# First layer of a four-layer kernel: the shift mask moved into q and k, the bias' third part added on the scores' row groups, and two VectorE steps written for ScalarE

## The reference

```python
B, DIM, HEADS, BLOCKS = (16, 48, 6, 6)
WS, SHIFT, MLP = (8, 4, 4)
...
def _block(x, shifted, n1g, n1b, qkvw, qkvb, pw, pb, rpb, n2g, n2b, f1w, f1b, f2w, f2b):
    shortcut = x
    x = _ln(x, n1g, n1b).reshape(B, H, W, DIM)
    if shifted:
        x = jnp.roll(x, (-SHIFT, -SHIFT), (1, 2))
    xw = _win_part(x)
    qkv = (xw @ qkvw.T + qkvb).reshape(-1, N, 3, HEADS, HD).transpose(2, 0, 3, 1, 4)
    q, k, v = (qkv[0], qkv[1], qkv[2])
    attn = jnp.einsum('bhnd,bhmd->bhnm', q * SCALE, k)
    attn = attn + rpb[RPI].transpose(2, 0, 1)[None]
    if shifted:
        attn = (attn.reshape(B, NW, HEADS, N, N) + MASK[None, :, None]).reshape(-1, HEADS, N, N)
    attn = jax.nn.softmax(attn, -1)
    xw = jnp.einsum('bhnm,bhmd->bnhd', attn, v).reshape(-1, N, DIM)
    xw = xw @ pw.T + pb
    x = _win_rev(xw)
    if shifted:
        x = jnp.roll(x, (SHIFT, SHIFT), (1, 2))
    x = shortcut + x.reshape(B, H * W, DIM)
    h = _ln(x, n2g, n2b)
    h = jax.nn.gelu(h @ f1w.T + f1b, approximate=False) @ f2w.T + f2b
    return x + h
```

## Time and profile before

| | us |
|---|---|
| median of 3 runs | 938.65 |
| the runs | 934.58, 942.16, 938.65 |
| the profiled execution | 939.39 |
| its span | 937.6 |
| TensorE busy | 766.7 (82%) |
| VectorE busy | 796.1 (85%) |
| ScalarE busy | 571.5 (61%) |
| GpSimd busy | 239.9 (26%) |

### The profile page before, as it was taken

How to read it: one execution, slowest core, us unless ns; L and a number is a source line. 1 busy time by engine, 2 the same in 40 slices (tenths; PEclk the granted TensorE clock), 3 DMA queues, 4 the chain that set the end, 5 groups by cost and what they waited for, 6 DMA issues and landing times.

```text
span 937.6 us, 20502 instructions
## 1 busy us (share of the span) xinstructions
PE 766.7 (82%) x7954; PEld 510.5 (54%) x7956; DVE 796.1 (85%) x2014; ACT 571.5 (61%) x854; POOL 239.9 (26%) x276
## 2 busy tenths in 40 slices
PE   2699999999999999999999978889877867432446
PEld 1467887777788777777777753376321111000113
DVE  7899999999989999998999964654449999999983
ACT  1387777787778777786777743133356666555142
POOL 6222222222222223222222221392121121212101
PEclk8699999999999999999999997887876765565577
DMA  8200000000000000002000000100002676657501
GB/s 233 72 2 3 1 2 2 1 2 2 2 2 2 2 2 2 2 2 108 3 2 1 2 1 1 50 1 1 1 1 51 119 140 129 123 114 135 101 0 34
DMA packets 11623, 34.14 MB, mean 36 GB/s; under 512 B 1879, under 2 KB 4359, under 8 KB 11271
## 3 DMA queue, kind: packets, MB, share of 16 engines
q0 software_dynamic: 5904, 21.24, 11.9%
q1 hardware_dynamic: 5623, 11.60, 4.2%
HBM read 10.81 MB, written 0.79 MB: 12 GB/s over the span
## 4 chain that ended last, share of the span: by engine, by line
PE 54%; DVE 30%; issue 5%; ACT 5%; DMA 2%; POOL 2%; POOLq 0%; DVEq 0%; another core or an unknown queue 0%; ACTq 0%
PE narrow L1524 7%; PE wide L1445 4%; PE scores_a L1505 4%; PE scores_b L1505 3%; DVE prod L1007 3%; DVE prod L1015 3%; PE last L1603 3%; PE wide L1589 3%; PE narrow L1554 2%; DVE mx L613 2%; PE last L1576 2%; PE narrow L1457 2%; DVE v L607 2%; PE scores_a L1494 2%; PE scores_a L1481 2%
## 5 line engine op out<-in xcount | busy, mean ns | idle before, releaser
L381 POOL TENSOR_TENSOR stb<-stb,neg_half 128x4 f32<-128x4 f32 x48 | 48.4, 1008 | 329.0 <-DVE stb L678 329.0
L1524 PEld LDWEIGHTS narrow<-v,pt 128*64 128x64 f32 x2304 | 82.1, 142 | 16.2 <-issue 16.2
L1133 ACT ACTIVATE d<-d 128x768 f32<-128x768 f32 x96 | 80.8, 841 | 16.4 <-DVE d L625 15.7
L1524 PE MATMUL narrow<-v,pt 128*64 128x54 f32 x2304 | 88.4, 229 | 0.0
L1787 PE MATMUL scores_b<-xb,gates_w 128*32 128x512 bf16 x192 | 26.0, 556 | 62.0 <-DVE yo L1027 52.9
L1149 ACT ACTIVATE ga<-wide 128x512 f32<-128x512 f32 x48 | 28.7, 597 | 66.1 <-PE wide L1589 66.1
L607 DVE COPY v<-narrow 64x96 f32<-64x96 f32 x192 | 49.1, 255 | 13.7 <-PE narrow L1457 11.0
L1157 ACT ACT_TABLE_LOAD x46 | 59.0, 1283 | 0.8
L1133 ACT ACT_TABLE_LOAD x46 | 59.0, 1283 | 0.8
L1445 PE MATMUL wide<-xa,wts 113*120 113x256 f32 x192 | 56.1, 416 | 0.8 <-ACT xa L1109 0.8
L376 POOL TENSOR_TENSOR sta<-sta,neg_half 128x4 f32<-128x4 f32 x48 | 53.0, 1105 | 12.8 <-DVE sta L566 12.8
(11 more groups left out here) (355 smaller groups left out, 2211.6 us busy)
## 6 DMA issues: line engine op xcount, KB each, us to landing
gsum<-mag POOLq DMA_DIRECT2D x14, 512.0 KB, 4.6
ysum<-yo POOLq DMA_DIRECT2D x7, 768.0 KB, 5.6
ysum<-xd POOLq DMA_DIRECT2D x6, 768.0 KB, 5.8
gsum<-mag POOLq DMA_DIRECT2D x14, 256.0 KB, 4.8
wts<-in_wpack SPq DMA_DIRECT2D x6, 442.0 KB, 7.2
sed_w<-in_sed_in SPq DMA_DIRECT2D x1, 2304.0 KB, 8.1
graw<-in_gates_in SPq DMA_DIRECT2D x1, 1152.0 KB, 4.9
x_all<-in_x_tok SPq DMA_DIRECT2D x8, 96.0 KB, 2.8
```

The lines of the kernel that those rows point to most:

```text
L381: pool.tensor_tensor(st[n % 2].stb[:, 1], st[n % 2].stb[:, 0], neg_half[:, 0:TILES], ALU.pow).then_inc(rstd2, 1)
L1133: act.activation(d, d, ACT.Exp).then_inc(p_ready[u], 1)
L1524: op = pe.matmul(y_ps[64 * b:64 * b + 64, q * VO:(q + 1) * VO], t.pt[:, q, h, 64 * b:64 * b + 64], t.v[:, q, b, h * VO:(h + 1) * VO], star ...
```

## The change

- **Mask.** Each shifted block's scores get -100 between regions from q and k themselves. `xa` has 8 more rows (113 to 120), one-hot region numbers loaded once per buffer by a small DMA (`mask_in`); the weights have 4 more columns per row group, so that q carries sqrt(8) (1 after its scale) for every region but the token's own and k carries -100 for its own. The q and k groups have 28 rows for 24. In unshifted blocks these weights are zero.
- **Third part of the bias.** `bias` keeps the matmul of `bias_hm`. The low part is made once per block in `bias_low` (64 rows), spread by 8 DMAs from SBUF to SBUF over four row groups of `bias_l`, and added by `bias_lows`: 16 matmuls of 32 rows by 64 columns right ahead of `scores`. No copy of the low part for the second half of an odd block, no mask rows, no memsets for them on GpSimd.
- **Steps moved.** `take_o` goes from VectorE to ScalarE, between `take_q` and the exponential of half b; `squares_a` from VectorE to ScalarE, behind `affine_a`, now three slots ahead, with the function Square.

The diff, cut to its core:

```diff
+            def spread_low(b):
+                w = 192 * (1 + b % 2)
+                sp.wait_ge(tables_done, b + 1)
+                for r in range(2):
+                    for u in range(2):
+                        for h in range(2):
+                            sp.dma_start(bias_l[64 * r + 32 * u:64 * r + 32 * u + 32, T_OFF[b] + h * w:T_OFF[b] + (h + 1) * w],
+                                         bias_low[32 * h:32 * h + 32, T_OFF[b] + r * w:T_OFF[b] + (r + 1) * w]).then_inc(ld_low, 16)
...
-            for dst, src in ((ident2[:], ident2_in), (fn_gb[:], fn_in), (perms[:], ident_in[:, 1:3])):
+            for dst, src in ((ident2[:], ident2_in), (fn_gb[:], fn_in), (perms[:], ident_in[:, 1:3]),
+                             *((t.xa[WIN:WIN + REG], mask_in) for t in st)):
                 sp.dma_start(dst, src).then_inc(ld_const, 16)
...
             load_rpb(1)
-            for b in (1, 3, 5):
-                sp.dma_start(bias_lm[64:128, L_OFF[b]:L_OFF[b] + 1536], mask_in).then_inc(ld_mask, 16)
+            spread_low(0)
...
-            sp.wait_ge(tables_done, BLOCKS)
+            for b in range(1, BLOCKS):
+                spread_low(b)
             sp.dma_start(sed_w[:], sed_in).then_inc(ld_sed, 16)
...
@@ -549,16 +556,6 @@
                 dve.scalar_tensor_tensor(w, wmean[:].unsqueeze(2).to_broadcast([128, 6, C]), -1.0 / C, w,
                                          ALU.mult, ALU.add).then_inc(centred, 1)
 
-            def squares_a(n):
-                if not live(n):
-                    return
-                t, x = st[n % 2], x_all[:, n % CHUNKS]
-                if n < CHUNKS:
-                    dve.wait_ge(emb_done, 4 * (0 if n < 1 else 1 if n < 4 else 2) + 4)
-                else:
-                    dve.wait_ge(x2_ready, n - CHUNKS + 1)
-                dve.scalar_tensor_tensor(t.sqa[:, :, 0:C], x, 1.0 / C, x, ALU.mult, ALU.mult).then_inc(sq1_done, 1)
-
             def variance_a(n):
                 if live(n):
...
@@ -642,13 +639,6 @@
                                   o[:, :, 0:C].rearrange("p q (h c) -> p q h c", c=HD),
                                   t.rd[:].unsqueeze(3).to_broadcast([128, 4, HEADS, HD]), ALU.mult).then_inc(on_ready, 1)
 
-            def take_o(n):
-                if live(n):
-                    dve.wait_ge(pe_oT, n + 1)
-                    if n >= 2:
-                        dve.wait_ge(pe_proj, n - 1)
-                    dve.tensor_copy(st[n % 2].oT[0:WIN], y_ps[0:WIN, 0:256]).then_inc(o_ready, 1)
-
             def add_proj(n):
 
...
@@ -727,10 +717,8 @@
             def table_low(b):
                 w = SC * (1 + b % 2)
                 dve.wait_ge(mid_done, b + 1)
-                for u in range(1 + b % 2):
-                    low = bias_lm[0:64, L_OFF[b] + w * u:L_OFF[b] + w * (u + 1)]
-                    op = dve.tensor_tensor(low, rpb_sb[:, T_OFF[b]:T_OFF[b] + w], low, ALU.subtract)
-                op.then_inc(tables_done, 1)
+                low = bias_low[:, T_OFF[b]:T_OFF[b] + w]
+                dve.tensor_tensor(low, rpb_sb[:, T_OFF[b]:T_OFF[b] + w], low, ALU.subtract).then_inc(tables_done, 1)
 
             dve.wait_ge(set_ln, 15)
...
@@ -769,13 +756,12 @@
                 if k == 52:
                     fill(2)
                     fill(3)
-                take_o(k - 4)
...
                                    ACT.Copy).then_inc(pt_ready[u], 1)
 
+            def take_o(n):
+                if live(n):
+                    act.wait_ge(pe_oT, n + 1)
+                    if n >= 2:
+                        act.wait_ge(pe_proj, n - 1)
+                    act.activation(st[n % 2].oT[0:WIN], y_ps[0:WIN, 0:256], ACT.Copy).then_inc(o_ready, 1)
+
+            def squares_a(n):
+                if not live(n):
+                    return
+                if n < CHUNKS:
+                    act.wait_ge(emb_done, 4 * (0 if n < 1 else 1 if n < 4 else 2) + 4)
+                else:
+                    act.wait_ge(x2_ready, n - CHUNKS + 1)
+                if n >= 2:
+                    act.wait_ge(var1, n - 1)
+                act.activation(st[n % 2].sqa[:, :, 0:C], x_all[:, n % CHUNKS], ACT.Square, scale=C ** -0.5).then_inc(sq1_done, 1)
...
-                for u in range(1 + b % 2):
-                    op = act.activation(bias_lm[0:64, L_OFF[b] + w * u:L_OFF[b] + w * (u + 1)], rest, ACT.Copy)
-                op.then_inc(mid_done, 1)
+                act.activation(bias_low[:, T_OFF[b]:T_OFF[b] + w], rest, ACT.Copy).then_inc(mid_done, 1)
 
             table_high(0)
             table_middle(0)
-            act.wait_ge(ld_const, 16 * 3)
+            squares_a(0)
+            act.wait_ge(ld_const, 16 * 5)
             for k in range(SLOTS + 4):
                 exponential(k - 2, 0)
                 take_q(k - 1)
+                take_o(k - 3)
                 exponential(k - 2, 1)
                 take_PT(k - 2, 0)
                 take_PT(k - 2, 1)
                 gelu_b(k - 4)
                 affine_a(k)
+                for n in (k + 3,) if k else (1, 2, 3):
+                    squares_a(n)
...
-                    op = pe.matmul(hid_bank[0:120, part, 0:256], w[0:WIN, col:col + 120], t.xa[0:WIN, :], start=True, stop=True)
+                    op = pe.matmul(hid_bank[0:124, part, 0:256], w[0:WIN + REG, col:col + 124], t.xa[0:WIN + REG, :], start=True, stop=True)
...
-                    for part in range(2):
...
-                        pe.matmul(dst, ident2[:], rhs, start=(part == 0), stop=(part == 1))
+                    if shifted(n):
+                        rhs = bias_hm[:, T_OFF[b] + SC * r:T_OFF[b] + SC * (r + 1)]
+                        dst = sc_bank[u][:, r, 0:SC]
+                    else:
+                        rhs = bias_hm[:, T_OFF[b] + 192 * r:T_OFF[b] + 192 * (r + 1)].unsqueeze(1).to_broadcast([128, 2, 192])
+                        dst = sc_bank[u][:, r, 0:SC].rearrange("p (v c) -> p v c", v=2)
+                    pe.matmul(dst, ident2[:], rhs, start=True, stop=True)
+
+            def bias_lows(n):
+
+                if not live(n):
+                    return
+                blk = n // CHUNKS
+                if n % CHUNKS == 0:
+                    pe.wait_ge(ld_low, 16 * 8 * (blk + 1))
+                for h in range(2):
+                    for b in range(2):
+                        for r in range(2):
+                            for u in range(2):
+                                g = 2 * r + u
+                                rows, off = slice(32 * g, 32 * g + 32), T_OFF[blk] + h * 192 * (1 + blk % 2)
+                                if shifted(n):
+                                    rhs = bias_l[rows, off:off + SC]
+                                    dst = sc_bank[u][64 * b:64 * b + 64, r, 0:SC]
+                                else:
+                                    rhs = bias_l[rows, off:off + 192].unsqueeze(1).to_broadcast([32, 2, 192])
+                                    dst = sc_bank[u][64 * b:64 * b + 64, r, 0:SC].rearrange("p (v c) -> p v c", v=2)
+                                first = 32 * (h != u)
+                                pe.matmul(dst, ident2[rows, first:first + 64], rhs, start=False, stop=True, skip_group_check=True)
...
-                                rows, cols = slice(64 * r + 32 * u, 64 * r + 32 * u + 24), slice(128 * v + 64 * b, 128 * v + 64 * b + 64)
+                                rows, cols = slice(64 * r + 32 * u, 64 * r + 32 * u + 28), slice(128 * v + 64 * b, 128 * v + 64 * b + 64)
                                 op = pe.matmul(sc_bank[u][64 * b:64 * b + 64, r, 192 * v:192 * v + 192], t.q[rows, cols], t.k[rows, :, cols],
                                                start=False, stop=True, skip_group_check=True)
...
                 windows_T(k)
+                bias_lows(k - 1)
                 scores(k - 1)
...
+            for r in range(2 * (l % 2)):
+                for g in range(4):
+                    row, at = WIN + 4 * u, 64 * r + 32 * u + 24 + g
+                    w[row:row + 4, W_Q + at] = HD ** 0.5
+                    w[row + g, W_Q + at] = 0.0
+                    w[row + g, W_K + at] = -100.0
```

66 lines of the change are left out of this document (26 added, 40 removed).

## The result

The changed kernel is slower. Its median is 949.4 us (947.95 to 952.51) against 936.62 (934.46 to 942.16) of the kernel before, ratio 1.0123 with a 95% interval of 1.0083 to 1.0162. Measured again later beside new runs of the kernel before (9 and 22 of them), it is 948.18 against 938.77, ratio 1.0099 (1.0067 to 1.0131). I had forecast 933.5, range 920 to 945. The profiled execution has a span of 948.4 us.

A forecast was written before the change was run, and what follows sets the result against it. It took two level loops, TensorE alone and TensorE with ScalarE, as the bound; +0.9 - 1.1 - 4.9 - 1.2 + 0.9 = -5.4 from the profiled 939.39 us gave 934.0, forecast 933.5 as a median, range 920 to 945.

The forecast's parts named there:

- ScalarE's part: Ordinary slot: `oT` delays half b's exponential by about 0.27, offsetting TensorE's saving; +0.03 in about 30 slots, +0.9 us.
- two loops of equal length: Ordinary slot of 10.49 us: one loop of TensorE alone, one going TensorE, ScalarE, TensorE, called level.
- TensorE's part: Each slot: four bias matmuls go, -0.65; 16 small ones come, eight together, +0.33; TensorE's own part falls by 0.32.
- Rival 2: The 16 low products go four at a time and take 0.65: +15 us, 949; chance 0.10.
- The ordinary slot: About 30 of the 48 slots: 0.03 longer each, +0.9 us; bounds -0.32 to +0.15 a slot.
- The low tables: Odd blocks: one subtraction for two saves 0.85 three times, two clock falls of 1.19 avoided; -4.9 us.
- The middle tables: Odd blocks: three ScalarE copies ahead of `xb` become two; -0.4 three times, -1.2 us.
- VectorE's part: 14 slots where VectorE ends last: losing `sqa` and `oT` gives -0.08 each, -1.1 us; ordinary slots 0.
- The square: On ScalarE between `xa` and `xb`: takes 0.33, 0.23 with overlap; free in an ordinary slot, no wait of VectorE.
- Rival 4: The square or the copy costs two table loads a slot on ScalarE: +125 us, 1058; chance 0.02.
- Rival 3: TensorE idle spots in ordinary slots lower the clock: 945 if ten slots fall once by 1.19; chance 0.08.
- Rival 1: TensorE's gain arrives in ordinary slots, half b's exponential not holding its transposes: -10.5 us more, 923; chance 0.17.

The follow-up runs named there:

- e8: The kernel before with only the window transposes written to a bank of `wide` instead of `narrow`; ratio 1.0002 to the kernel before.
- e6: The kernel before with only the copy `oT` and square a moved to ScalarE, its tables and mask as before; ratio 1.008 to the kernel before.
- e9: The changed kernel with the low products ahead of the window transposes and the copy `oT` back on VectorE, the square still on ScalarE; 929.74 us.
- e7: The changed kernel with the window transposes in a bank of `wide` and the copy `oT` back on VectorE; 924.84 us.
- e1: The changed kernel with the 16 low products put ahead of the window transposes instead of behind them; 940.36 us.
- e4: The changed kernel with the window transposes written to the first bank of `wide` instead of `narrow`, both moved steps staying on ScalarE; 930.72 us.
- e3: The changed kernel with each of the four first bias matmuls issued twice in every slot; 941.7 us.
- e5: The changed kernel with the copy `oT` and square a both back on VectorE, leaving the new tables, regions and low products; ratio 0.9988 to the kernel before.
- e11: The changed kernel with the four first bias matmuls issued twice in chunks 44 to 47 only; 947.11 us.

## Why the prediction was wrong

**The failed step** is in ScalarE's part, in the words "The window transposes now end at 210.64 + 0.27 - 0.65 = 210.26, so they hold nothing". I let them move forward by the 0.65 of the removed matmuls, without asking what else they wait for. They wait for `v_ready`, and the copies of `v` end at 210.08, 0.15 ahead of their start. So the four removed matmuls could give nothing there (a wait of 0.60 took the place of their 0.65), and the 16 low products, put behind the wait, are a pure addition of 0.27 (0.35 from their start at 214.69 to the first score product at 215.04, less 0.08, since from there to the transposes of `zb` it is 215.80 - 215.04 = 0.76 for 211.41 - 210.57 = 0.84 before). With these two terms put right, the prediction's own sum for TensorE at the transposes of `zb` is 211.42 + 0.27 + 0.27 = 211.96, 0.54 later than before, and 0.54 is what a slot grew by. The picture of "two loops of equal length" lacked the third: TensorE projects `v`, VectorE copies it, TensorE transposes. It was as long as the others, and e8 shows that it was even the longest, by 0.15.

**Point by point.**
- TensorE's part, +0.33 for 16 matmuls eight at a time: right (0.35, of which 0.27 stays). Eight start within 0.02 us, the next eight 0.19 behind the first (214.69, 214.88). Rival 2 (four at a time), 949 us, comes near the measured time by chance; its mechanism did not happen. The rule of the Trainium skill behind it ("TensorE: Matmul & The Clock Gate", Part 3: a weight load overlaps running matmuls only on another row group) is not borne out: here two products on each row group start together, and all 16 weight loads start between 214.69 and 214.74, the second eight while the first eight products run.
- The copy `oT` delays the exponential of half b by 0.27: right in size. From `q` to the exponential it is 0.28 before and 0.55 after (210.48 - 209.93). But I set it off against TensorE's saving; with no saving it is lost whole: e6, +0.27.
- The ordinary slot: forecast +0.03 in 30 slots, 0.9 us. Measured +0.54, which is 24.3 us if 45 slots are counted. This term is the error; part of it, 16.7 us, came back because longer slots no longer stand out, where I had forecast 4.9 + 1.2 + 1.1 = 7.2.
- The low tables: forecast -4.9, with both falls of the clock avoided. Between kernels with the same ordinary slot (before and e9) it is -5.6. Right in sign, and 0.7 more. In the changed kernel `zb` is not waited for there any more; VectorE's subtraction and TensorE in that slot:

```profile
258.65 0.95 DVE L721 TENSOR_TENSOR bias_low<-sed_w,bias_low 64x768 bf16<-64x768 f32 x1
...
260.22 0.44 PE L1590 MATMUL narrow<-ident,zb 128*128 128x128 f32 x2
...
262.49 1.77 PE L1547 MATMUL narrow<-v,pt 128*64 128x54 f32 x48
```

  The matching rows before have 1.05 of idle time and 2.96.
- The middle tables: forecast -1.2. Between before and e9 the three distances where an odd block's are made (the 1st, 17th and 33rd) give -0.75. VectorE's part: forecast -1.1 in 14 slots; -1.2 in the last nine distances and some -2 in other slots, nearly all of it in the 9th, 12th, 16th, 25th, 28th and 32nd distance. Both right in sign, the first too large, the second a third of what came.
- The square: free, as forecast (0.35 on ScalarE, no wait of VectorE in the ordinary slot, 46 loads of each table in both kernels). Rival 4 is out.
- The start: forecast +0.9. The first GELU is at 52.59 against 52.56, and at 53.13 when the changed kernel was profiled again: no delay that can be told from the spread.
- The eight DMAs per block: forecast 0. No wait of TensorE for them has a row between 60 and 555 us.
- Rival 3 (the clock falls in ordinary slots): didn't happen, 1.00 from 100 to 200 us although TensorE idles 0.60 in each slot.
- Rival 1 (TensorE's gain arrives): 923, with slots of 10.2. It did not happen. e7 comes near it (924.84, 10.19), but by another bank, by `oT` on VectorE, and with VectorE setting most of these slots, so the agreement is chance.

The chances were wrong in kind: I had no rival for a wait in the place where I subtracted 0.65.

## What to carry to other kernels

Before work of an engine is subtracted, list every semaphore that its next instruction waits for, and when each is raised: what is taken away in front of a wait that is nearly level gives nothing, and its row of waits is empty in the trace of before. The same place tells where added work is free: ahead of the wait (e1), not behind it. And where loops are level, a single edit can show nothing: the bank alone gave no change of the median (e8), with the removed matmuls it gave 0.8% (e4), and with the copy back on VectorE too 1.6% (e7). A length that fits a sum can still be set by another engine (10.19 in e7): look at which row the next one follows.

## What the runs showed of the hardware

- 32-row by 64-column matmuls on eight tiles start within 0.02 us of one another and take 0.19 and 0.16 us for two rounds of 384 bf16 columns (starts at 214.69, 214.88, and the next product at 215.04), though two share each row group.
- An idle time of 1.38 us on TensorE was followed by a lower granted clock in one execution of the changed kernel and not in the next (value products of 2.97 and 1.77). In the kernel before, 1.03 was followed by 1.77 in one slot and 1.05 by 2.96 in another. Forty-three idle times of 0.60, one every 11 us, left the clock at 1.00.
- Outside the blocks, equal programs differ: from the 46th GELU to the end of the launch the profiled executions took, with nearly the same code there, from 387 to 399 us, while ordinary slots repeat to 0.01 us. In the 100 us behind the 48th GELU the granted clock is 0.91 in the executions that take 356 to 358 us from there (e3, e4, e5, e11) and 0.85 in those that take 360 to 362 (the kernel before and the changed one among them; e9 lies between, 0.88 and 358). A question of 0.3 us a slot is answered by one trace, not by medians.
